# Another order of steps in each engine's program of the stage of layers 1 and 2

## The reference

```
x = x + L0_xattn(norm(x), ctx)      # 16 heads of 16, causal
x = x + L0_ffn(norm(x))             # 8 experts, each takes its top tokens
x = x + L1_xattn(norm(x), ctx)      # 16 heads of 64; of each row of scores the 32 largest
x = x + L1_ffn(norm(x))             # 1.58-bit weights, 8-bit rows, 256 -> 1024 -> 256
x = x + L2_xattn(norm(x), ctx)      # 16 heads of 64, plain softmax
x = x + L2_ffn(norm(x))             # rows rounded to FP8, 256 -> 256
x = x + L3_xattn(norm(x), ctx)      # one head, causal
x = x + L3_ffn(norm(x))             # top 2 of 8 experts and a shared one
```

## Time and profile before

| | before |
|---|---|
| time, median of 3 runs | 3299.59 us |
| span of the profiled execution | 3339.0 us |
| PE busy | 2950.2 us (88%) |
| DVE busy | 2569.5 us (77%) |
| ACT busy | 2342.2 us (70%) |
| POOL busy | 2125.1 us (64%) |
| mean granted TensorE clock | 0.961 |

### The profile page before, as it was taken

How to read it: one execution, slowest core, us unless ns; L and a number is a source line. 1 busy time by engine, 2 the same in 40 slices (tenths; PEclk the granted TensorE clock), 3 DMA queues, 4 the chain that set the end, 5 groups by cost and what they waited for, 6 DMA issues and landing times.

```text
span 3339.0 us, 63437 instructions
## 1 busy us (share of the span) xinstructions
PE 2950.2 (88%) x19271; PEld 2153.9 (65%) x19271; DVE 2569.5 (77%) x9486; ACT 2342.2 (70%) x7209; POOL 2125.1 (64%) x3576
## 2 busy tenths in 40 slices
PE   7888887969979999999989999999999896997984
PEld 5666564537756777777667776667667554764873
DVE  5666565638999999999999999999999854552334
ACT  6777631107989999999989999999999873331111
POOL 5666502436877898888888788888888752015125
PEclk9999998989999999999999999999999998996997
DMA  3310144453100000000000000000000011002887
GB/s 128 114 62 22 57 149 135 131 152 99 54 20 4 1 12 8 9 12 8 9 22 8 9 12 20 11 8 13 8 19 12 30 43 47 20 20 95 251 261 249
DMA packets 145177, 195.58 MB, mean 59 GB/s; under 512 B 13219, under 2 KB 119228, under 8 KB 144700
## 3 DMA queue, kind: packets, MB, share of 16 engines
q1 hardware_dynamic: 132422, 166.35, 15.6%
q0 software_dynamic: 12288, 25.18, 2.8%
q10 hardware_dynamic: 128, 0.00, 0.0%
HBM read 127.38 MB, written 62.53 MB: 57 GB/s over the span
## 4 chain that ended last, share of the span: by engine, by line
DVE 33%; PE 25%; ACT 14%; issue 6%; POOL 6%; DMA 1%; another core or an unknown queue 1%; POOLq 1%; SPq 0%; ACTq 0%; DVEq 0%
DVE s_W L1460 7%; DVE s_W L1464 5%; PE ps L902 3%; DVE s_W L1446 3%; DVE s_W L1442 3%; DVE s_W L1451 3%; DVE s_W L1477 3%; PE ps L2792 2%; PE ps L2781 2%; POOL s_W L1380 2%; ACT s_W L1560 2%; PE ps L918 2%; ACT s_W L1578 1%; PE ps L1663 1%; ACT s_W L1569 1%
## 5 line engine op out<-in xcount | busy, mean ns | idle before, releaser
L1380 POOL TENSOR_SCALAR s_W<-s_W 128x256 f32<-128x256 f32 x512 | 586.5, 1146 | 62.5 <-ACT s_W L1552 14.6
L1460 DVE MATCH_REPLACE8 s_W<-s_W 128x256 f32<-128x256 f32 x1024 | 409.6, 406 | 0.0
L1384 POOL TENSOR_TENSOR s_W<-s_W 128x256 f32<-128x256 f32 x512 | 380.3, 764 | 20.5
L1663 PE MATMUL ps<-s_W 64*128 64x256 f32 x2048 | 338.4, 414 | 59.6 <-ACT s_W L1525 17.4
L1464 DVE MAX8 s_W<-s_W 128x8 f32<-128x256 f32 x1024 | 379.2, 410 | 0.0
L1676 PE MATMUL ps<-s_idf,s_W 128*128 128x128 f32 x2048 | 330.8, 284 | 46.7 <-ACT s_W L1569 41.0
L1676 PEld LDWEIGHTS ps<-s_idf,s_W 128*128 128x128 f32 x2048 | 220.4, 141 | 197.0 <-issue 139.9
L1586 ACT ACTIVATE s_W<-ps 128x512 f32<-128x512 f32 x512 | 315.6, 617 | 3.7 <-PE ps L1676 1.5
L1578 ACT ACTIVATE s_W<-ps,s_W 128x256 f32<-128x256 f32 x512 | 243.6, 496 | 78.9 <-DVE s_W L1477 78.3
L366 POOL TENSOR_SCALAR s_W<-s_W 128x128 f32<-128x128 f32 (+1 forms) x512 | 209.6, 429 | 120.2 <-DVE s_W L403 120.0
L1560 ACT ACTIVATE s_W<-s_W 128x256 f32<-128x256 f32 x512 | 262.0, 528 | 27.9 <-POOL s_W L1384 22.5
(11 more groups left out here) (398 smaller groups left out, 7925.7 us busy)
## 6 DMA issues: line engine op xcount, KB each, us to landing
s_W<-in_ctxT SPq DMA_DIRECT2D x82, 256.0 KB, 2.8
s_RA<-in_L_expert SPq DMA_DIRECT2D x36, 514.0 KB
s_W<-keys_values SPq DMA_DIRECT2D x114, 128.0 KB, 2.2
s_RC<-in_L_expert SPq DMA_DIRECT2D x18, 514.0 KB
keys_values<-s_W SPq DMA_DIRECT2D x33, 256.0 KB, 2.0
s_RC<-expert_in SPq DMA_DIRECT2D x31, 256.0 KB
keys_values<-s_RC SPq DMA_DIRECT2D x24, 256.0 KB, 2.0
expert_in<-s_W SPq DMA_DIRECT2D x4, 1280.0 KB, 6.2
```

Of the source, the lines that this page charges most:

```text
L1380: at.append(g.did(g.e.tensor_scalar(cm[:, h, :], sc[:, h, :], sm[:, 48 + 8 * h + 7:48 + 8 * h + 8], NEG, ALU.is_lt, ALU.mult)))
L1384: g.e.tensor_tensor(cm[:, h, :], cm[:, h, :], sc[:, h, :], ALU.add).then_inc(sig("cut"), 1)
L1460: cut_at.append(v.did(v.e.match_replace(out=cut[:, h, :], in_to_replace=m8[rnd][h], in_values=cut[:, h, :], imm_value=-3e38)))
L1663: i = mm(out[:, h, 0:256], q[64 * h:64 * h + 64, :], k[64 * h:64 * h + 64, :], start=True, stop=not first)
```

## The change

The table `TIMES` gets other numbers, 82 of its 89 over the five engines; the steps, their functions, the instructions and what each waits for are the same, but for the banks, which follow PE's order. `TIMES3`, of the last phase, is as it was.

```diff
--- before.py
+++ after.py
@@ -2021,30 +2021,26 @@
 
 
 TIMES = {
-    "pe": {"late": -6, "c1.turn_x": -3.107, "c1.qk": -1.643, "c1.scores": 0.089, "c1.turn": 4.286,
-           "c1.values": 4.352, "c1.pv": 5.872, "c1.project": 6.31,
-           "c2.turn_x": -2.542, "c2.qk": -1.458, "c2.early": -1.423, "c2.scores": 0.166, "c2.values": 0.695,
-           "c2.turn": 2.896, "c2.pv": 4.859, "c2.project": 6.078,
-           "f1.turn": 25.841, "f1.up": 26.33, "f1.back": 30.799, "f1.down": 32.343,
-           "f2.turn": 31.721, "f2.out": 38.351},
-    "act": {"late": -6, "c1.turn_x": -3.637, "c1.qk": -1.749, "c1.scores": -0.071, "c1.best": 1.107,
-            "c1.keep": 2.908, "c1.scale": 3.779, "c1.turn": 4.043, "c1.values": 4.134, "c1.pv": 5.816,
-            "c2.turn_x": -2.75, "c2.qk": -1.926, "c2.early": -1.14, "c2.scores": 0.054, "c2.values": 0.27,
-            "c2.turn": 2.867, "c2.pv": 4.347,
-            "f1.turn": 25.397, "f1.up": 26.069, "f1.quant": 27.94, "f1.back": 30.6,
-            "f2.turn": 31.142},
-    "dve": {"late": 0, "c1.mask": -22, "c1.measure": -17.059, "c1.select": 0.95, "c1.best": 1.054,
-            "c1.weights": 3.086, "c1.add": 21.196,
-            "c2.scores": 0.029, "c2.inverse": 0.959, "c2.add": 20.082,
-            "f1.norm": 23.183, "f1.in": 24.128, "f1.up": 26.942, "f1.quant": 27.771, "f1.quant2": 29.801,
-            "f1.down": 32.666,
-            "f2.norm": 24.42, "f2.scale": 24.842, "f2.round": 28.405, "f2.round2": 30.549, "f2.out": 38.226},
-    "pool": {"c1.measure": -17.002, "c1.norm": -5.668, "c1.remove": 2.136, "c1.blend": 3.071, "c1.add": 21.738,
-             "c2.norm": -3.7, "c2.scale": 1.637, "c2.turn_x": 4.29, "c2.add": 20.901,
-             "f1.norm": 22.793, "f1.down": 33.044,
-             "f2.norm": 23.507, "f2.out": 40.133},
-    "sp": {"weights": -21.867, "late": -6, "reload": 0, "c1.fetch": -4.754, "c1.load_k": -1.072, "c1.load_v": 4.175,
-           "c2.early": -1.354, "c2.fetch": -1.2, "c2.load_k": -0.627, "c2.early_fetch": -0.546, "c2.load_v": 4.918},
+    "pe": {"late": -6, "c1.turn_x": -2.823, "c1.qk": -1.578, "c1.scores": 0.039, "c1.turn": 4.316, "c1.values": 3.664,
+           "c1.pv": 5.826, "c1.project": 6.969, "c2.turn_x": -3.24, "c2.qk": -1.812, "c2.early": 1.721,
+           "c2.scores": -0.078, "c2.values": 1.17, "c2.turn": 2.806, "c2.pv": 4.384, "c2.project": 5.276,
+           "f1.turn": 26.262, "f1.up": 26.418, "f1.back": 30.685, "f1.down": 31.14, "f2.turn": 34.91,
+           "f2.out": 37.944},
+    "act": {"late": -6, "c1.turn_x": -3.266, "c1.qk": -1.745, "c1.scores": -0.195, "c1.best": 0.949, "c1.keep": 2.685,
+            "c1.scale": 3.754, "c1.turn": 4.012, "c1.values": 3.285, "c1.pv": 5.735, "c2.turn_x": -3.442,
+            "c2.qk": -1.931, "c2.early": 2.006, "c2.scores": -0.059, "c2.values": 0.801, "c2.turn": 2.588,
+            "c2.pv": 4.191, "f1.turn": 25.941, "f1.up": 26.181, "f1.quant": 28.853, "f1.back": 30.369,
+            "f2.turn": 34.356},
+    "dve": {"late": 0, "c1.mask": -22, "c1.measure": -23.499, "c1.select": 0.486, "c1.best": 1.012,
+            "c1.weights": 3.258, "c1.add": 21.039, "c2.scores": -0.124, "c2.inverse": 0.927, "c2.add": 19.248,
+            "f1.norm": 24.179, "f1.in": 25.134, "f1.up": 26.835, "f1.quant": 28.65, "f1.quant2": 30.009,
+            "f1.down": 31.484, "f2.norm": 25.228, "f2.scale": 27.959, "f2.round": 31.823, "f2.round2": 32.548,
+            "f2.out": 37.952},
+    "pool": {"c1.measure": -18.917, "c1.norm": -7.078, "c1.remove": 1.645, "c1.blend": 2.531, "c1.add": 22.222,
+             "c2.norm": -5.986, "c2.scale": 0.837, "c2.turn_x": -1.709, "c2.add": 20.219, "f1.norm": 23.307,
+             "f1.down": 31.183, "f2.norm": 22.723, "f2.out": 51.964},
+    "sp": {"weights": -21.867, "late": -6, "reload": 0, "c1.fetch": -4.431, "c1.load_k": 6.755, "c1.load_v": 10.892,
+           "c2.early": -0.153, "c2.fetch": 8.897, "c2.load_k": 9.192, "c2.early_fetch": 0.46, "c2.load_v": 11.354},
 }
```

## The result

The kernel after takes 3422.03 us, the median of 4 runs (3419.21 to 3424.34), beside 3299.95 us of the kernel before on the same chip: the ratio is 1.0364, 95% interval 1.035 to 1.0379. That is 122 us slower, where 11 faster was predicted, and 100 above the top of the range.

The account below looks back on a forecast made before the run. The prediction took VectorE's work plus a little idling as the bound. Head -6, layer 2's scores -7 and tile changes +2 made -11 us, from 3299.6 to 3288.6, with a range of 3269 to 3322.

Parts of the forecast that it names:

- The head, -6.0: Start of the stage: statistics ahead of the mask and early groups behind the second scores start layer 1 6.0 us sooner.
- An earlier start stays in the time: After the head: VectorE is the bound from there on, so the 6.0 us gained are kept.
- the two edits: In the head: batch 0's statistics ahead of the mask, 3.2 us sooner; early groups behind the second scores, 3.5 us.
- VectorE's and GpSimd's order, 0: Steady cycle: one exchange on VectorE, a pure shift on GpSimd; cost 0, bounds -1 and +3 us.
- TensorE, the scores of layer 2, -7 of 14.6: Steady part: layer 2's scores ahead of layer 1's recover 7 of VectorE's 14.6 us of waiting for them.
- Tile changes, +2: TensorE, steady part: more tile-shape changes add 47 us of its time, mostly under idling; 2 us reach the end.
- ScalarE, 0 with -5 and +10: ScalarE's steady order, including layer 2's values copy behind the pv that frees its buffer: 0, bounds -5 and +10 us.
- SyncE, 0: Transfer queue: loads issued later by the table still go out early enough; cost 0, up to 13 us if queued longer.
- the tail, 0: End of the stage: same steps remain, TensorE busy 94.7%; 0, bounds -6 and +3 us.
- The rivals: Whole kernel: everything recoverable comes, 3274 (0.17); only the head stays and is eaten up, 3299 (0.20); slower, 3322 (0.23).
- The slower one: Slots with an f1 tile: tile changes make TensorE the bound, delaying layer 2's scores; 3322, at worst 3341; chance 0.23.

Follow-up runs that it names:

- the head alone, batch 0 only: Kernel before with batch 0's statistics 6.5 slots earlier and layer 2's early groups three slots later: ratio 1.0013.
- the first alone: Kernel before with only batch 0's statistics 6.5 slots earlier, ahead of the mask, early groups left in place: ratio 0.9991.
- the converse run: Kernel before, all orders kept, the banks of layer 2's scores counted as handed out two places earlier, so reused sooner: ratio 1.0658.
- The split alone: Kernel before with layer 2's pv moved from 4.859 to 4.68 on TensorE, so a values product separates most pv pairs: ratio 1.0026.
- joining the groups: Kernel after with both layers' pv together and layer 2's scores right behind layer 1's on TensorE: ratio 1.0276 without other edits.
- due banks: Kernel after, each TensorE step taking the bank whose last content is read earliest by the tables, not the one handed out longest ago: ratio 1.0096.
- moved values: Kernel after with ScalarE's copy of layer 2's values moved behind layer 2's exponentials: ratio 1.0201 alone, 1.0089 with banks by due reading too.
- the two traces with 7.15 us an item: Kernel before with batch 0's statistics earlier, once with the early groups three slots later (ratio 1.0013), once without (0.9991).
- the kernel before with due banks: Kernel before, orders kept, each TensorE step taking the bank whose last content is read earliest by the tables: ratio 1.0319.

## Why the prediction was wrong

*What bounds the kernel.* "VectorE's work plus a little idling" was right of the kernel before and was wrongly kept for the kernel after. The argument ran that other engines' idling costs nothing until it reaches VectorE; true, but three engines over 93% leave 0.2 to 0.5 us a slot, and the change makes a ring through all of them that takes 8.12 us where VectorE's own work takes 7.4 (1451.77 / 197).

*The head, -6.0.* Right at its place, -6.05: statistics at 740.93, ahead of the mask at 744.17, and first MAX8 at 755.75. Rows of the kernel after:

```profile
740.93 0.43 DVE L201 BATCH_NORM_STATS2 s_st<-s_x 128x6 f32<-128x256 f32 x1 [0.56 <-DMA s_x<-acc_rows]
744.17 0.20 DVE L1425 TENSOR_SCALAR s_W<-s_W 128x8 f32<-128x8 f32 x1 [2.06 <-DMA s_W<-mask_tiny]
753.64 1.22 PE L1663 MATMUL ps<-s_W 64*128 64x256 f32 x4 [0.90 <-ACT s_W L1525]
755.75 0.75 DVE L1442 MAX8 s_W<-s_W 128x8 f32<-128x256 f32 x2 [3.37 <-ACT s_W L1545]
```

Two sub-steps were off. "An earlier start stays in the time" failed: with the head alone, batch 0 only, none of 6.7 us stayed (1.0013). And the two edits don't add as 3.2 and 3.5: the first alone brings 1.4, as the context is in its way while the early groups are.

*VectorE's and GpSimd's order, 0.* I looked at the steady cycle and not at the steps once a batch. `measure` no longer stands between two steps of `f1`; on the kernel before that brings 18 us of waiting on L1788 (1.0066 against 1.0013 without it). In the kernel after the same wait is 2.0 us, since `f1` has moved too, so there it is no part of the loss.

*TensorE, the scores of layer 2, -7 of 14.6.* This is the step that failed: the wait at L1477, which the prediction had fall under 8 us, became 126.5. It took "issued earlier in TensorE's list" for "done earlier". What stood ahead of the scores in the list had in the meantime been given banks that are freed late. The front of this text says that `Banks` follows TensorE's order; the prediction moved that order and gave the banks no term. By the lists, between slots 43 and 256, the steps that take a bank whose last content is the layer 2 scores just ahead are: `c1.turn` 0 before, 74 after; `c1.qk` 12 before, 72 after. The trace has 57 waits at the turns and 67 at the queries' products. Put shortly, the two layers' scores have changed places, and with them the distance after which their banks are taken again: before, 4 or 5 places for layer 1's, which one copy frees, and 5 to 8 for layer 2's, which are free only after VectorE's maximum and ScalarE's exponentials; after, nearly the other way about. The run with other banks and nothing else gives back 2.7 points, 88 us of 3300, and the converse run shows that banks alone can cost 221.

*Tile changes, +2.* The price on TensorE was of the right size. For `pv` it was 25 us for 105 splits, 0.24 each, and the split alone measures 0.1 to 0.19 each. For all tile changes it was 0.22 us a slot, and joining the groups takes off 0.26 (7.41 to 7.15), with due banks 0.21 (7.28 to 7.07), with due banks and moved values 0.31 (7.33 to 7.02). What was mis-sized is the share that reaches the end. The split alone costs 0.26%, 9 us; with the banks by due reading, joining the groups gives back 0.65 points without the moved values (1.0096 to 1.0031) and 0.92 with it (1.0089 to 0.9997), 21 to 30 us. Not all of this need be the splits, since joining the groups gives some steps other banks as well; that isn't told apart.

*ScalarE, 0 with -5 and +10.* Wrong in size and in sign of the argument. I called the later `c2.values` a gain, as it stands behind the `pv` that frees its buffer. But it now stands ahead of layer 2's exponentials, and its product comes late on TensorE: 93.1 us of waiting at L1539. Taken back alone it gives 1.6 points, after the banks none, after banks and joined groups 0.3. With the groups joined the wait at L1539 is small by itself, 8.5 us, and another has come at L1592.

*SyncE, 0, and the tail, 0.* Right. From 1000 to 2600 us no engine's wait names a transfer, the transfers of the earlier trace rows land as fast, and from the last MAX8 on the tail takes 2.8 us more.

```profile
s_W<-in_ctxT SPq DMA_DIRECT2D x82, 256.0 KB, 2.8
...
s_W<-keys_values SPq DMA_DIRECT2D x114, 128.0 KB, 2.1
```

*The rivals.* The slower one had the right sign, and 3341 at its worst. Its mechanism, TensorE saturated by tile changes in the slots of `f1`, isn't what happened: TensorE has 0.29 us more work for an item, but it isn't saturated, as its idle time in the long stretch rose from 105 to 140 us. The tile changes are at most the smaller part of the loss, 0.65 to 0.92 points of 3.64.

## What to carry to other kernels

When an order is changed, list what else is computed from it. Here the banks follow TensorE's order, and a step that inherits a bank inherits the whole chain up to the read of its last content; look in both orders how many places further on a bank is taken again, and how long the chain is that frees it; the number of steps that take a bank of one kind isn't enough. With several engines over 90%, price a change by the ring that it closes, and not by the engine that is busiest. An engine's wait for an instruction whose result it doesn't use is the mark of a shared buffer.

## What the runs showed of the hardware

The price of a split was measured in place: 97 more groups that use 64 columns of the array between groups that use all of it made TensorE busy for 18.55 us longer in 1600, at the same number of items, 0.19 us for each; against the two traces with 7.15 us an item it is 0.1. From start to start a group of eight such products takes 1.01 us in the trace of the split, and two in a row 1.88 in the trace before (medians of 192 and 93), so 0.14 for a split. It is between 0.1 and 0.2 us.

The first scores of the stage, four products of L1663, take 1.22 us in the kernel after (753.64, 15.5 us after the first transfer; mean granted clock of 720 to 760 us 0.57, so part of it at the lower level of 1.2 GHz). In the run with batch 0's statistics and the early groups moved, the same four products start 15.5 us after the first transfer as well (752.96) and take 0.70. From 752 to 757 us the granted clock reads 0.50 in the first, the lower level, and 0.93 in the second. TensorE's work ahead of them is alike (a turn, queries and keys from 747.04 and from 746.37 on), so in these two runs it doesn't fix the instant at which the clock rises, and half a microsecond at such a head is luck.

In the kernel before with due banks TensorE's waits reach 3.9 us, and the granted clock of the long stretch reads 0.95 instead of 0.99:

```profile
1000.00:2600.00 1600.00, 1453.90 (x9468) 1078.57 (x9468) 1470.53 (x5667) 1413.95 (x4278) 1256.81 (x2011) 0.95 0.03 10
```

That makes its busy time no longer comparable by itself: 7.38 us for each of 197 items, where the kernel before has 7.12 for the same instructions. The converse run, with waits as long and TensorE less busy (1372.77 us), reads 0.97, so the busy share doesn't order the two.
